# Graph attention on one core: Q rows fetched from DRAM by group, a one-hot made by a matmul of distance features, a ring of 16 gathered groups, and edge features loaded two groups at a time

## The chip, the cores and the metric

The kernel runs on one core of one Trainium2 chip. The metric is the time of one execution on the device, in microseconds (us). The kernel before takes 2109.49 us, the median of three runs (2108.01 to 2111.33). A core has five engines with instruction streams of their own: TensorE (PE; PEld is its weight load), VectorE (DVE), ScalarE (ACT), GpSimd (POOL) and SyncE (SP), which here only issues transfers. They wait for each other through semaphores.

## The reference

One graph attention layer with edge features, a residual and a layer norm. There are 6250 nodes with 128 features, 8 heads of 16, and 206250 edges sorted by their destination `dst` (33 per node on average).

```python
Q, K, V = x @ WQ, x @ WK, x @ WV            # 6250 x 128
E = edge_attr @ WE                          # 206250 x 128
score = exp(clip(sum_d(K[src] * Q[dst] * E) / 4, -5, 5))   # per edge and head
wV = segment_sum(V[src] * score, dst);  Z = segment_sum(score, dst)
out = layernorm(x + wV / (Z + 1e-6))
```

## The kernel before, in words

**Tiling.** Edges are taken in groups of 512 (4 tiles of 128), 403 groups (`G`). Nodes are cut into 49 windows of 128 (`WIN`). As the edges are sorted, a group's destinations lie close together, and the kernel finds a place for each group from its first edge: a window that starts at a multiple of 64 nodes.

**Prologue.** Twelve chunks of four windows and one of a single window. Per chunk SP loads x (`load_x`), TensorE transposes it and forms K and V (`kv_products`, L507), VectorE copies them out (`copy_kv`, L816), SP stores them to `kv_table` in DRAM (L321, L324). SP's order is: four x chunks, `dst`, two index loads (L274), four edge loads (L284), then per chunk the next x and the store. Between the copies VectorE works on `dst` (`place_first_edges`, L848; `place_groups`). TensorE turns the local destinations (`turn_local`), then forms Q chunk by chunk (`q_products`); ScalarE and VectorE split each Q chunk into three bf16 parts (L693, L832, L699, L836) kept in SBUF as `Qp`, and SP moves halves of it so that `Qp` has windows at multiples of 64 (`move_q`).

**GpSimd.** After the stores of `kv_table` it does nothing but gathers: per group four indirect transfers of 128 rows of K and V, 1 KB each (`gather`, L444), into `kv[:, g % 8]`. The ring has 8 slots (`RINGS`), and the gather of group g waits for the messages of group g - 8 (`msg_ok`).

**The main loop**, each engine in a fixed order written out in `step`:

- SP: edge features of a group, 256 KB (`load_attr`, L284; four buffers), once in eight groups the indices, once in eight groups the store of a finished window.
- TensorE, step g: turn the edge features of g+2 (`turn_attr`, L545), turn the one-hot of g+2 (`turn_hot`, L564), E of g+1 (`edge_products`, L554), Q of g+1 by the turned one-hot times three parts of `Qp` (`select_q`, L577: 12 matmuls), sums of g-1 (`sum_messages`, L588).
- ScalarE, step g: copy the turned features (L734) and the turned one-hot (L741) of g+2, the exponentials of g (L748), the one-hot of g+3 as `relu(1 - |place - node| * 2)` (`mark`, L721 four times and L726).
- VectorE, step g: K times E (L916, which waits for the gather), the sums of g-2 added to `acc` (L955 twice), times Q (L921), the messages of g-1 (L938, which reads `kv` and `msg`), the reduction to scores (L926), the clipping (L932), and in between single stages of a finished window (`finish`).

**Tail.** The last four windows are finished and stored. If a group reached beyond its place, a redo part with loops follows, which is skipped with this graph.

Of the kernel before, what the change touches and what calls it, by code (L numbers as in the profile page):

```python
# [15 lines left out]
RINGS = 8  # L16
HOTS = 5
MSGS = 2
XBUFS = 4
ATTRS = 4  # L20
LAG = 5
BIG = 1.0e6
HALF_WINDOW, SLOT, ODD_BIT, STRAYS, FIRST, OPEN = range(6)
COLUMN = (1, 3, 1)
NOT_AN_EDGE = 0.5
# [12 lines left out]
def graph_attention_layernorm(nc, x, src, dst, edge_attr, wq, wk, wv, we, out):  # L38
# [21 lines left out]
    ODD = WIN - 1  # L60
    SLOTS = WIN + ODD
# [8 lines left out]
    B_LAST = G // RINGS  # L70
    EARLY = B_LAST - LAG
    LATE = WIN - EARLY
    RES_WIN = -(-(WIN - 1) // RINGS)
    STAGES = 10 + 3 * NEWTON_STEPS
    assert STAGES <= 3 * RINGS and 0 < LATE <= TILES
# [3 lines left out]

    q_odd_dmas = sum((c * CW < ODD) + 1 for c in range(CH))  # L80

# [4 lines left out]
    kv_table = nc.dram_tensor("kv_table", [n_nodes, 2 * dim], F32).ap()  # L86

    with ExitStack() as ctx:
# [12 lines left out]
        table = sb("table", [1, 6, -(-(G + max(COLUMN)) // 4) * 4], I32)  # L101
        xT = sb("xT", [P, WIN * P])
        acc = sb("acc", [P, WIN, MW])
        Qp = sb("Qp", [P, SLOTS, 3, dim], BF16)
        kv = sb("kv", [P, RINGS, TILES, 2 * dim])
        src_idx = sb("src_idx", [P, 2, RINGS, TILES], U32)
# [3 lines left out]
        hotT = sb("hotT", [P, 2, GROUP], BF16)  # L110
        prod = sb("prod", [P, GROUP])
# [4 lines left out]
        home = sb("home", [P, GC * P])  # L116
        iota = sb("iota", [P, 2, P])
        ident = sb("ident", [P, P])
        w_e = sb("w_e", [P, dim])
        pair_col = sb("pair_col", [P, GC], I32)  # L120
        int_cols = sb("int_cols", [P, GC, 3], I32)
        place_cols = sb("place_cols", [P, GC, 3])
        home_col = sb("home_col", [P, GC])
        ones_col = sb("ones_col", [P, 1], BF16)
        one = sb("one", [P, 1])
        cur = sb("cur", [P, 2, TILES])
# [10 lines left out]
        w_kv = hot[:, XBUFS, 0:2, :].rearrange("p t d -> p (t d)")  # L137
        w_q = hot[:, XBUFS, 2, :]
        x_last = prod[:, 0:dim]
        q_rest = attrT[:, :, :]  # L140
        least = msg[:, 0, :, :].rearrange("p t m -> p (t m)")[:, 0:G]
        most = msg[:, 1, :, :].rearrange("p t m -> p (t m)")[:, 0:G]
        place_rows = hotT[0:3, :, :].rearrange("r s e -> r (s e)").bitcast(I32)[:, 0:G]
        stray_row = most[0:1, :]
        stray = prod[:, dim:2 * GROUP // 2].bitcast(BF16)[:, 0:G]
# [3 lines left out]
        rows = Qp[:, :, :, :].rearrange("p s t d -> p (s t d)").bitcast(F32)[:, SLOTS * 3 * dim // 2 - GC * GROUP:]  # L149
        dst_rows = rows.bitcast(I32).rearrange("p (c e) -> p c e", c=GC)  # L150
        local_rows = rows.rearrange("p (c e) -> p c e", c=GC)
        psT = pb("psT", [P, GROUP])
        psH = pb("psH", [P, GROUP])
# [3 lines left out]
        psX = [psT, psH]  # L157
        turn_bank = [psQ[:, 0, :], psQ[:, 1, :], psT[:, :], psH[:, :]]
# [4 lines left out]
        id_zero = sem("id_zero")  # L163
        const_ready = sem("const_ready")
# [4 lines left out]
        x_at = [sem(f"x_at{i}") for i in range(XBUFS)]  # L169
        prep = sem("prep")  # L170
        masked = sem("masked")
        turned = sem("turned")
# [6 lines left out]
        kv_out = sem("kv_out")  # L179
        kv_stored = [sem(f"kv_stored{i}") for i in range(RINGS)]  # L180
# [5 lines left out]
        q_odd = sem("q_odd")  # L186
        x_pad = sem("x_pad")
        x_res_in = sem("x_res_in")
        range_ok = sem("range_ok")
        stray_ok = sem("stray_ok")  # L190
        stray_mm = sem("stray_mm")
# [3 lines left out]
        idx_in = [sem(f"idx_in{i}") for i in range(2)]  # L195
        idx_end = sem("idx_end")
        attr_in = [sem(f"attr_in{i}") for i in range(ATTRS)]
# [7 lines left out]
        hot_tr = sem("hot_tr")  # L205
# [18 lines left out]
        s_ke = sem("s_ke")  # L224
        s_cur = sem("s_cur")
        s_hot = sem("s_hot")
        s_hot_tr = sem("s_hot_tr")
        s_hotT = sem("s_hotT")
        s_q = sem("s_q")
        s_keq = sem("s_keq")  # L230
        s_dot = sem("s_dot")
        s_clip = sem("s_clip")
        s_exp = sem("s_exp")
        s_msg = sem("s_msg")
        s_sums = sem("s_sums")
# [21 lines left out]
        def _(sp):  # L257
# [11 lines left out]
            def load_indices(b):  # L269
                if b >= 2:  # L270
                    for u in range(RINGS):
                        sp.wait_ge(kv_in[u], (b - 1) * TILES * 16)
                first, n = b * RINGS, min(RINGS, G - 1 - b * RINGS)
                sp.dma_start(src_idx[:, b % 2, 0:n, :], src[first * GROUP:(first + n) * GROUP]  # L274
                             .rearrange("(u p t) -> p u t", u=n, p=P).bitcast(U32)).then_inc(idx_in[b % 2], 16)
                if n < RINGS:
                    sp.dma_start(src_idx[:, b % 2, n, :], src[n_edges - GROUP:n_edges]
                                 .rearrange("(p t) -> p t", p=P).bitcast(U32)).then_inc(idx_end, 16)

            def load_attr(b, u):  # L280
                g = b * RINGS + u
                if past(g, ATTRS):
                    sp.wait_ge(attr_tr, g - ATTRS + 1)
                sp.dma_start(attr[:, u % ATTRS, :, :], edge_attr[bass.ds(edge0(g), GROUP), :]  # L284
                             .rearrange("(p t) d -> p t d", p=P)).then_inc(attr_in[u % ATTRS], 16)

# [11 lines left out]
            load_indices(0)  # L298
            load_indices(1)
            for u in range(ATTRS):  # L300
                load_attr(0, u)

            def move_q(c):

                w0, n = c * CW, chunk_windows(c)
                sp.wait_ge(q_lo, c + 1)
                up = min(w0 + n, ODD)
                if up > w0:
                    sp.dma_start(Qp[HALF:P, WIN + w0:WIN + up, :, :], Qp[HALF:P, w0:up, :, :]).then_inc(q_odd, 16)
# [818 lines left out]
```

## Time and profile before

| | |
|---|---|
| median of three runs | 2109.49 us (2108.01 to 2111.33) |
| the profiled execution's own time | 2111.6 us |
| its span, first to last instruction | 2109.8 us |
| mean granted TensorE clock | 0.981 of full |
| first gather starts, last starts | 47.3 us, 2086.7 us |
| bytes moved | 342.89 MB, 163 GB/s on average |
| queue of the gathers, queue of SP | 34.8% and 21.6% of 16 DMA engines |

The page gives the busy time of each engine and its share of the span, then the chain that ended last: the work followed back from the last instruction, at each step to what released it. In groups of instructions the columns are: line, engine, operation, written tile and read tiles, count, busy time and mean ns of one, then the idle time of the engine just before them and what ended most of it. "issue" is time in which an engine waited for nothing that the profile shows.

### The profile page before, as it was taken

The page shows a single profiled execution, that of the slowest core. Times are in us where ns is not written, and L with a number is a line of the kernel's source. Part 1 is how long each engine was busy: PE and PEld are TensorE (multiplying, and loading weights), DVE is VectorE, ACT ScalarE, POOL GpSimd, SP SyncE. Part 2 cuts the span into 40 slices and gives each one's busy share as a digit, 9 for nine tenths or more (in the row PEclk, how much of TensorE's full clock was granted, in tenths as well). Part 3 has the DMA queues.
Part 4 walks back from the last instruction along what each step waited for, and adds up shares of the span by engine and source line. Part 5 has one row for each costly group of instructions (what it writes and reads, how often), then busy time and mean ns, then how long its engine had stood idle before and what let it go on. Part 6 is the DMA issues. An engine that isn't in the chain of part 4 may idle for free.

```text
span 2109.8 us, 49493 instructions
## 1 busy us (share of the span) xinstructions
PE 1560.1 (74%) x14786; PEld 1436.8 (68%) x14787; DVE 1487.4 (70%) x3785; ACT 1317.4 (62%) x3270; POOL 1558.1 (74%) x1628
## 2 busy tenths in 40 slices
PE   8678777777777777777776777777777777777775
PEld 6577777677667666767666766666666667676674
DVE  4777677667767767767776776776777777677666
ACT  2667666666656666666666666666666666666663
POOL 2777777777777777777777777777777777777774
PEclk9899999989999999999999999999999999999998
DMA  7965555555555555555555555555555555555552
GB/s 236 272 176 165 161 162 161 156 158 160 154 164 157 159 162 156 161 159 158 162 159 159 157 159 160 160 161 160 157 163 158 158 162 152 162 161 159 160 156 82
DMA packets 217419, 342.89 MB, mean 163 GB/s; under 512 B 86480, under 2 KB 112056, under 8 KB 217163
## 3 DMA queue, kind: packets, MB, share of 16 engines
q0 software_dynamic: 77376, 211.39, 34.8%
q1 hardware_dynamic: 139211, 128.05, 21.6%
q8 instruction: 132, 2.16, 0.4%
q14 instruction: 124, 1.02, 0.2%
q10 hardware_dynamic: 576, 0.26, 0.0%
HBM read 325.24 MB, written 9.60 MB: 159 GB/s over the span
## 4 chain that ended last, share of the span: by engine, by line
POOL 40%; issue 20%; DVE 11%; PE 11%; DMA 8%; ACT 5%; DVEq 4%; SPq 1%; POOLq 0%
POOL kv L444 40%; DMA kv<-kv_table,src_idx 7%; PE psW L588 4%; DVE msg L938 3%; ACT hot L721 3%; DVEq L247 3%; DVE acc L955 3%; PE psE L554 2%; PE psQ L577 2%; DVE prod L921 2%; ACT hot L726 2%; PE psH L564 2%; DVE score L926 1%; DVEq L955 1%; PE psE L507 1%
## 5 line engine op out<-in xcount | busy, mean ns | idle before, releaser
L444 POOL DMA_INDIRECT kv<-kv_table,src_idx x1612 | 1549.6, 961 | 513.3 <-issue 495.7
L916 DVE TENSOR_TENSOR prod<-kv,psE 128x512 f32<-128x512 f32 x403 | 276.5, 686 | 472.9 <-DMA kv<-kv_table,src_idx 284.5
L588 PE MATMUL psW<-msg,hot 128*128 128x136 f32 x3224 | 473.6, 290 | 111.3 <-DVE msg L938 111.1
L564 PE MATMUL psH<-ident,hot 128*128 128x128 f32 x1612 | 264.8, 288 | 332.3 <-ACT hot L726 327.2
L721 ACT ACTIVATE hot<-iota,local 128x128 f32 x1612 | 508.8, 386 | 2.0 <-issue 1.5
L588 PEld LDWEIGHTS psW<-msg,hot 128*128 128x128 f32 x3224 | 406.5, 192 | 132.2 <-DVE msg L938 130.9
L564 PEld LDWEIGHTS psH<-ident,hot 128*128 128x128 f32 x1612 | 175.0, 142 | 411.3 <-ACT hot L726 410.6
L554 PE MATMUL psE<-w_e,attrT 128*128 128x128 f32 x3224 | 432.1, 278 | 0.0
L748 ACT ACTIVATE msg<-clipped 128x32 f32<-128x32 f32 x403 | 92.3, 229 | 522.4 <-DVE clipped L932 515.1
L554 PEld LDWEIGHTS psE<-w_e,attrT 128*128 128x128 f32 x3224 | 398.1, 194 | 0.0
L577 PE MATMUL psQ<-Qp,hotT 128*128 x4836 | 340.1, 221 | 8.9 <-DMA Qp<-Qp 8.9
L577 PEld LDWEIGHTS psQ<-Qp,hotT 128*128 128x128 bf16 x4836 | 308.6, 99 | 14.2 <-issue 9.2
L734 ACT ACTIVATE attrT<-psT 128x512 f32<-128x512 f32 x403 | 235.6, 585 | 114.9 <-PE psT L545 98.1
L545 PE MATMUL psT<-ident,attr 128*128 128x128 f32 x1612 | 247.3, 277 | 71.7 <-issue 71.7
L726 ACT ACTIVATE hot<-hot,one 128x512 f32<-128x512 f32 x403 | 290.8, 722 | 13.1
L955 DVE TENSOR_TENSOR acc<-psW,acc 64x136 f32 x806 | 237.7, 295 | 79.0 <-PE psW L588 68.3
L741 ACT ACTIVATE hotT<-psH 128x512 bf16<-128x512 f32 x403 | 240.2, 596 | 83.5 <-PE psH L564 81.9
L921 DVE TENSOR_TENSOR prod<-prod,psQ 128x512 f32<-128x512 f32 x403 | 277.4, 688 | 17.1 <-PE psQ L577 4.5
L938 DVE TENSOR_TENSOR msg<-kv,msg 128x512 f32<-128x512 f32 x403 | 276.9, 687 | 0.3 <-ACT msg L748 0.3
L926 DVE TENSOR_REDUCE score<-prod 128x32 f32<-128x512 f32 x403 | 271.2, 673 | 0.0
L545 PEld LDWEIGHTS psT<-ident,attr 128*128 128x128 f32 x1612 | 192.0, 143 | 80.2 <-issue 80.2
L932 DVE TENSOR_SCALAR clipped<-score 128x32 f32<-128x32 f32 x403 | 89.0, 221 | 4.6
(94 smaller groups left out, 352.7 us busy)
## 6 DMA issues: line engine op xcount, KB each, us to landing
attr<-in_edge_attr_dram SPq DMA_DIRECT2D x403, 256.0 KB
kv<-kv_table,src_idx POOLq DMA_INDIRECT x1612
kv_table<-kv SPq DMA_DIRECT2D x12, 512.0 KB, 4.0
Qp<-Qp SPq DMA_DIRECT2D x23, 192.0 KB
hot<-in_x_dram SPq DMA_DIRECT2D x12, 256.0 KB, 4.7
xT<-in_x_dram SPq DMA_DIRECT2D x8, 384.0 KB
out_dram<-xT SPq DMA_DIRECT2D x45, 64.0 KB
src_idx<-in_src_dram SPq DMA_DIRECT2D x50, 16.0 KB
```

The costliest lines, as they stand in the source:

```text
L444: nc.gpsimd.indirect_dma_start(out=kv[:, u, t, :], out_offset=None, in_=kv_table, in_offset=bass.IndirectOffsetOnAxis(ap=src_idx[:, b % 2, ...
L545: last = nc.tensor.transpose(psT[:, t * P:(t + 1) * P], attr[:, u % ATTRS, t, :], ident[:, :])
L554: last = nc.tensor.matmul(psE[:, u % 2, t * P:(t + 1) * P], attrT[:, u % 2, t * P:(t + 1) * P], w_e[:, :], start=True, stop=True)
L564: last = nc.tensor.transpose(psH[:, t * P:(t + 1) * P], hot[:, g % HOTS, t, :], ident[:, :])
L577: last = nc.tensor.matmul(psQ[:, u % 2, t * P:(t + 1) * P], hotT[:, u % 2, t * P:(t + 1) * P], Qp[:, bass.ds(slot, 1), part, :].rearrange( ...
L588: last = nc.tensor.matmul(psW[:, u % 2, 0:MW], hot[:, g % HOTS, t, :], msg[:, g % MSGS, t, :], start=(t == 0), stop=(t == TILES - 1))
L721: last = nc.scalar.activation(hot[:, g % HOTS, t, :], nodes, ACT.Abs, scale=-1.0, bias=local[:, t, bass.ds(g, 1)])
L726: nc.scalar.activation(slot, slot, ACT.Relu, scale=-1.0 / NOT_AN_EDGE, bias=one[:, 0:1])\
L921: nc.vector.tensor_tensor(prod[:, :], prod[:, :], psQ[:, u % 2, :], ALU.mult).then_inc(keq, 1)
L926: nc.vector.tensor_reduce(score[:, :], prod[:, :].rearrange("p (a d) -> p a d", d=DH), AX.X, ALU.add)\
L938: nc.vector.tensor_tensor(per_head(msg[:, g % MSGS, :, 0:dim]), per_head(kv[:, u, :, dim:2 * dim]), msg[:, g % MSGS, :, dim:MW].unsqueeze( ...
L955: last = nc.vector.tensor_tensor(where, psW[half, u % 2, 0:MW], where, ALU.add)
```

## The change

It is one change with these parts:

- `Qp` in SBUF goes. Q's three bf16 parts of a chunk are made in `q_stage` (3 buffers) and stored to `q_table` in DRAM, where the part k of node n is row 3n + k. SP loads for each group the 128 rows from its base node on (`load_near_q`, 32 KB, a ring of 4 with the address from a register): 42 nodes by 3 parts.
- The turned one-hot for Q is no longer turned from `hot`. For each edge a row of three features is stored in DRAM: n = dst - base, and n squared in two bf16 parts. One bf16 matmul with constant coefficients gives 2jn - n^2 in partition 3j + k, and ScalarE makes it a one-hot: `relu(that + 1 - j^2)`. `select_q` needs 4 matmuls, as the sum over the parts is inside the matmul. `turn_hot` goes, the one-hot for the sums is marked for g+2 (4 buffers), and edges outside of the 42 nodes are marked as strays when the features are made.
- The ring of gathered groups has 16 slots, and `src_idx` holds the indices of all groups.
- K and V are staged in `kv_stage` (4 buffers); ScalarE copies every second pair of windows.
- In SP's order, index loads and edge loads stand after the stores of chunks 9 and 10 of K and V. `acc` is zeroed by VectorE after the Q stage, not by GpSimd at the start.
- The edge features of two groups are one transfer of 512 KB into two of six buffers.

```diff
-RINGS = 8
-HOTS = 5
-ATTRS = 4
+TURN = 8
+RINGS = 16
+NEAR = 42
+QROWS = 4
+FEATS = 4
+HOTS = 4
+ATTRS = 6
@@ sync
+            def load_attr_pair(g):
+                n = min(2, G - g)
+                if g >= ATTRS:
+                    sp.wait_ge(attr_tr, g - ATTRS + 2)
+                sp.dma_start(attr[:, g % ATTRS:g % ATTRS + n, :, :], edge_attr[edge0(g):edge0(g) + n * GROUP, :]
+                             .rearrange("(u p t) d -> p u t d", u=n, p=P)).then_inc(attr_in[g // 2 % (ATTRS // 2)], 16)
+            def load_near_q(g, base):
+                if g >= QROWS:
+                    sp.wait_ge(q_sel, g - QROWS + 1)
+                sp.dma_start(q_near[:, g % QROWS, :], q_rows[bass.ds(base, P), :]).then_inc(q_in[g % QROWS], 16)
+            def load_feats(k):
+                if k >= 2:
+                    sp.wait_ge(feat_mm, (k - 1) * FEATS)
+                sp.dma_start(feats[:, k % 2, :, :], near_table[k * FEATS:(k + 1) * FEATS, :, :]
+                             .rearrange("g f e -> f g e")).then_inc(feats_in[k % 2], 16)
...
+                if c == CH - 4:
+                    for b in range(3):
+                        load_indices(b)
+                elif c == CH - 3:
+                    for g in range(0, ATTRS, 2):
+                        load_attr_pair(g)
...
+            def load_group(g):
+                nonlocal bases
+                if g >= ATTRS and g % 2 == 0:
+                    load_attr_pair(g)
+                if g % FEATS == FEATS - 1 and 2 <= (g + 1) // FEATS <= (G - 1) // FEATS:
+                    load_feats((g + 1) // FEATS)
+                if g % TURN == 0 and g // TURN + 2 <= B_LAST:
+                    load_indices(g // TURN + 2)
+                if g > QROWS:
+                    if (g - 1) % TURN == 0:
+                        bases = load_bases(g - 1, min(TURN, G - g + 1))
+                    load_near_q(g - 1, bases[(g - 1) % TURN])
@@ tensor
-                for t in range(TILES):
-                    last = nc.tensor.transpose(psH[:, t * P:(t + 1) * P], hot[:, g % HOTS, t, :], ident[:, :])
+                nc.tensor.matmul(psF[:, :], coef[:, :], feats[:, g // FEATS % 2, g % FEATS, :], start=True, stop=True)\
+                    .then_inc(feat_mm, 1)
...
-                    for part in range(3):
-                        last = nc.tensor.matmul(psQ[:, u % 2, t * P:(t + 1) * P], hotT[:, u % 2, t * P:(t + 1) * P],
-                                                Qp[:, bass.ds(slot, 1), part, :].rearrange("p a d -> p (a d)"),
-                                                start=(part == 0), stop=(part == 2))
+                    last = nc.tensor.matmul(psQ[:, g % 2, t * P:(t + 1) * P], hotT[:, g % 2, t * P:(t + 1) * P],
+                                            q_near[:, g % QROWS, :], start=True, stop=True)
@@ scalar
-                nc.scalar.activation(hotT[:, u % 2, :], psH[:, :], ACT.Copy).then_inc(hotT_ok, 1)
+                nc.scalar.activation(hotT[:, g % 2, :], psF[:, :], ACT.Relu, bias=near_bias[:, 0:1]).then_inc(hotT_ok, 1)
...
+                if CH - 8 <= c < CH - 4:
+                    near_features(c - (CH - 8))
+                elif c >= CH - 4:
+                    square_high(c - (CH - 4))
@@ vector
+            for c in range(CH):
+                copy_kv(c)
+                if c == 1:
+                    find_bases()
+                elif c == 2:
+                    find_main(0)
+                elif c == 3:
+                    find_main(1)
+                elif c == 4:
+                    keep_main()
+                elif c == 5:
+                    find_places(0)
+                elif c == 6:
+                    find_places(1)
+                elif c == 7:
+                    keep_places()
+                elif c == 8:
+                    place_groups()
```

`find_main` to `keep_places` are single operations over 128 x 2048 elements, `find_bases` four over 128 x 512 and some small ones, `place_groups` a reduction over 128 x 2048 and small ones. `near_features` is two ScalarE operations over 128 x 512, `square_high` one.

## Rows read from the trace of the kernel before

**Rows 1.** The page: engines' busy time; then the chain's shares by engine.
```profile
PE 1560.1 (74%) x14786; PEld 1436.8 (68%) x14787; DVE 1487.4 (70%) x3785; ACT 1317.4 (62%) x3270; POOL 1558.1 (74%) x1628
...
POOL 40%; issue 20%; DVE 11%; PE 11%; DMA 8%; ACT 5%; DVEq 4%; SPq 1%; POOLq 0%
POOL kv L444 40%; DMA kv<-kv_table,src_idx 7%; PE psW L588 4%; DVE msg L938 3%; ACT hot L721 3%; DVEq L247 3%; DVE acc L955 3%; PE psE L554 2%; PE psQ L577 2%; DVE prod L921 2%; ACT hot L726 2%; PE psH L564 2%; DVE score L926 1%; DVEq L955 1%; PE psE L507 1%
```

**Rows 2.** The group of L444 on the page; its durations (ns min/median/max) from its line.
```profile
L444 POOL DMA_INDIRECT kv<-kv_table,src_idx x1612 | 1549.6, 961 | 513.3 <-issue 495.7
...
L444 POOL DMA_INDIRECT kv<-kv_table,src_idx x1612: 942/946/1462, 47.3 to 2086.7; - x180
```

**Rows 3.** Timeline, last two gathers: start us, us, what, [idle before <-releaser].
```profile
2085.41 0.94 POOL L444 DMA_INDIRECT kv<-kv_table,src_idx  x1 [0.30 <-issue]
...
2086.66 1.13 POOL L444 DMA_INDIRECT kv<-kv_table,src_idx  x1 [0.30 <-issue]
```

**Rows 4.** Windows: stretch and length, PE, PEld, DVE, ACT, POOL, PEclk, DMA share, GB/s.
```profile
90.00:100.00 10.00, 8.65 (x91) 8.30 (x89) 7.09 (x15) 7.91 (x21) 7.57 (x9) 1.00 1.07 313
400.00:800.00 400.00, 299.25 (x2838) 276.13 (x2837) 283.05 (x739) 253.57 (x632) 303.69 (x317) 0.97 0.55 158
```

**Rows 5.** Waits, whole span: who waited for whom, us in total, times, longest.
```profile
DVE prod L916 <- DMA kv<-kv_table,src_idx: 284.5, 203, 4.0
...
DVE acc L955 <- PE psW L588: 68.3, 77, 2.2
...
POOL kv L444 <- DVE msg L938: 17.7, 58, 0.3
```

**Rows 6.** Timeline of the prologue.
```profile
6.43 4.95 SPq L284 DMA_DIRECT2D attr<-in_edge_attr_dram  x4
...
17.13 0.82 PE L527 MATMUL psT<-ident,hot 128*128 128x128 f32 x4 [2.07 <-DMA hot<-in_x_dram]
...
17.74 3.46 PE L507 MATMUL psE<-hot,xT 128*128 128x256 f32 x8
...
22.45 1.67 DVE L848 TENSOR_SCALAR Qp<-Qp,home_col 128x512 f32<-128x512 int32 x4
...
24.87 1.97 PE L507 MATMUL psE<-hot,xT 128*128 128x256 f32 x8 [1.07 <-DVE kv L816]
...
29.28 1.89 PE L507 MATMUL psE<-hot,xT 128*128 128x256 f32 x8
...
31.44 1.89 PE L507 MATMUL psE<-hot,xT 128*128 128x256 f32 x8
...
47.30 1.11 POOL L444 DMA_INDIRECT kv<-kv_table,src_idx  x1 [22.41 <-issue]
```

**Rows 7.** The page's groups of the turned one-hot and the Q products.
```profile
L564 PE MATMUL psH<-ident,hot 128*128 128x128 f32 x1612 | 264.8, 288 | 332.3 <-ACT hot L726 327.2
...
L577 PE MATMUL psQ<-Qp,hotT 128*128 x4836 | 340.1, 221 | 8.9 <-DMA Qp<-Qp 8.9
```

**Rows 8.** The stores of kv_table (tile kv_table): from issue to landing.
```profile
DMA to landing us min/median/max: 2.9/4.0/6.8
```

**Rows 9.** Timeline: L938, and the gather that starts while it runs.
```profile
489.69 0.68 DVE L938 TENSOR_TENSOR msg<-kv,msg 128x512 f32<-128x512 f32 x1
...
489.76 1.44 POOL L444 DMA_INDIRECT kv<-kv_table,src_idx  x1 [0.30 <-issue]
...
1005.51 0.69 DVE L938 TENSOR_TENSOR msg<-kv,msg 128x512 f32<-128x512 f32 x1
...
1006.04 0.98 POOL L444 DMA_INDIRECT kv<-kv_table,src_idx  x1 [0.30 <-issue]
```

**Rows 10.** Timeline: durations on VectorE, for the prices.
```profile
30.34 0.69 DVE L816 COPY kv<-psE 128x512 f32<-128x512 f32 x1 [0.61 <-PE psE L507]
...
71.76 0.58 DVE L885 SCALAR_TENSOR_TENSOR prod<-msg 128x403 bf16<-128x403 f32 x1
```

**Rows 11.** Windows, columns as in rows 4: a sparse stretch.
```profile
425.00:430.00 5.00, 2.88 (x16) 2.48 (x17) 4.92 (x14) 2.60 (x7) 3.78 (x5) 0.71 0.48 132
```

More of the change, by code:

```diff
@@ L358, in _ @@
                     .then_inc(x_res_in, 16)
-            for b in range(2, LAG + 2):
+            for b in range(3, LAG + 2):
                 load_turn(b)
@@ L450, in _ @@
-            for u in range(RINGS):
-                gather(0, u)
-            for b in range(1, B_LAST):
-                for u in range(RINGS):
-                    gather(b, u)
-            for g in range(B_LAST * RINGS, G):
-                gather(g // RINGS, g % RINGS)
+                        out=kv[:, g % RINGS, t, :], out_offset=None, in_=kv_table,
+                        in_offset=bass.IndirectOffsetOnAxis(ap=src_idx[:, g, t:t + 1], axis=0))\
+                        .then_inc(kv_in[g % RINGS], 16)
@@ L459, in _ @@
+            for i in range(KV_STAGES):
+                pool.wait_ge(kv_stored[i], 16 * len(range(i, CH, KV_STAGES)))
+            for g in range(G):
+                gather(g)
             pool.wait_ge(table_ok, 1)
@@ L632, in _ @@
+            select_q(0)
+            for g in range(G):
+                step(g)
+            sum_messages(G - 1)
             pe.wait_ge(table_ok, 1)
@@ L862, in _, with find_main @@
-            for pair in range(-(-WIN // 2)):
-                copy_kv(pair)
-                if pair == 7:
-                    place_first_edges()
-                elif pair == 11:
+            def find_main(half):
+                dve.wait_ge(prep, 3 + half)
+                if half == 0:
+                    nc.vector.tensor_scalar(main, near, 0.0, None, ALU.is_ge).then_inc(prep, 1)
+                else:
+                    nc.vector.scalar_tensor_tensor(main, near, float(NEAR - 1), main, ALU.is_le, ALU.mult)\
+                        .then_inc(prep, 1)
@@ L867, in _ @@
                     place_groups()
+            for c in range(GC):
+                square_low(c)
             dve.wait_ge(turned, 2)
@@ L954, in add_sums @@
                     where = acc[half, bass.ds(w, 1), :].rearrange("p a m -> p (a m)")
-                    last = nc.vector.tensor_tensor(where, psW[half, u % 2, 0:MW], where, ALU.add)
+                    last = nc.vector.tensor_tensor(where, psW[half, g % 2, 0:MW], where, ALU.add)
                 last.then_inc(added, 1)
@@ L1033, in _ @@
[L1033 to L1038 removed]
+                windows = load_windows(b * TURN - 2, TURN)
+                for u in range(TURN):
+                    step(b * TURN + u, windows[u], b - LAG)
@@ L1039, in _ @@
+            windows = load_windows(B_LAST * TURN - 2, G - B_LAST * TURN + 2)
+            for g in range(B_LAST * TURN, G):
+                step(g, windows[g - B_LAST * TURN])
+            messages(G - 1)
+            add_sums(G - 2, windows[-2])
+            add_sums(G - 1, windows[-1])
             dve.wait_ge(added, G)
```

689 lines of the change are left out of this document (332 added, 357 removed).

## The prediction

> **What bounds the kernel now.** I read the engines' shares first, then the chain that ended last, then the gathers' own group. The shares settle nothing: TensorE 74%, GpSimd 74%, VectorE 70% [rows 1]. The chain does: 40% of it is one GpSimd line, L444, the indirect gathers of K and V rows, and 20% is "issue", time in which an engine waited for nothing [rows 1]. The group of L444 says whose issue time that is: 1612 gathers of 961 ns, and before them 513.3 us of idle time, of which 495.7 us are issue [rows 2]. In the order of time the gathers start every 1.25 us: 0.94 or 0.95 us of work and 0.30 us until the next [rows 3]. Four gathers make one group of 512 edges, so GpSimd needs 5.01 us a group, 403 times. A stretch of 400 us holds 317 of them, 1.262 us apiece [rows 4]: no pause is left in it. Line L444 waited for VectorE's messages 58 times, but never over 0.3 us, which is the pause it has anyway [rows 5]. So the ring of 8 slots is never full at GpSimd's cost, from the first gather at 47.30 [rows 6] to the last at 2086.66 [rows 3]. VectorE waits for landings (284.5 us) inside a cadence that GpSimd sets [rows 5].
>
> The span is therefore three terms: 47.3 us until the first gather, 2040.5 us of gathers (2086.66 + 1.13 - 47.30), and 22.0 us of tail. The profiled execution's own time is 2111.6 for a span of 2109.8; the median of the three timed runs is 2109.49, that is 2.1 below it. I work on the span and subtract 0.3.
>
> **TensorE's and ScalarE's edits: nothing.** Per group the four turns of the one-hot (L564, 264.8 us in all) go, and the twelve Q matmuls of L577 (340.1 us in all, 0.84 us a group) become four, about 0.28 us [rows 7]. What comes is one bf16 matmul of 512 columns on 3 rows: no row has this shape; four L577 matmuls cover 512 columns in 0.28 us, and twice that is the bound for the lower clock. TensorE goes from 1560.1/403 = 3.87 us a group to 3.87 - 0.66 - 0.56 + 0.28 = about 2.9. ScalarE keeps its count: the copy of L741 becomes a Relu of the same size. None of it lies on the cadence, so its worth is 0. If the cover went it would still only help. The register loads that these two lose go to SP, once in eight groups, where 40 us stand against them.
>
> **Ring of 16, index array for all groups: nothing.** They remove a wait that costs 0 now. They do cover more: 16 groups are 80 us instead of 40.
>
> **Q rows and features from DRAM.** SP issues per group one Q load (128 rows of 256 B) and half an edge transfer, per four groups a feature load. SP's wait for a Q slot is for the Q selection four groups back, and behind it in SP's order stand edge features, indices and stores. Loads have some three groups, 15 us, to land; kv stores land in 4.0 us by the median, 6.8 at most [rows 8]. Price 0, and 0 to 1 us a group if they came late, of which VectorE's slack takes 0.9. The DMA share is 0.55 in the steady stretch and was 1.07 at 90 to 100 us, where GpSimd was busy 7.57 us in 10, as elsewhere (303.69 in 400) [rows 4]: the issue of a gather does not suffer from a full DMA system. Its landing may, by some tenths of a us, and that leads to the next term.
>
> **The stretch of the gathers: +8 us.** The gathers' median is 946 ns, their mean 961, their maximum 1462 [rows 2]. The difference is 24 us over 1612, and it has one look: a gather that starts while VectorE runs L938 (both inputs in SBUF) is stretched. Started 0.07 us after L938 it took 1.44 us; 0.53 us after, 0.98 [rows 9]. The gather seems to be held until about 0.56 us after L938 began: 0.49 us are added at 0.07, 0.03 at 0.53.
>
> The Trainium skill ("GPSIMD Engine Reference", Key points) says that GpSimd shares its SBUF interfaces with VectorE, and that instructions with two SBUF inputs contend. The trace agrees with 0.2 to 0.5 us for a hit. By the rule alone the change is neutral, since L938 is not edited; what the sum takes is from the rows.
>
> What changes is where in the 1.25 us cadence L938 falls. It starts about 2 us after L916, and L916 starts when the group's last gather has landed. Evenly spread, 0.56/1.25 = 45% of groups would be hit for 0.28 us on average: 403 x 0.126 = 51 us. Now it is 24, so the present phase is a favourable one. Extra DMA traffic shifts landings later by a little and spreads them, and VectorE loses waits of L955 for TensorE (68.3 us in 77 [rows 5]), which moves L938 earlier by 0.9 us in a fifth of the groups. Both push towards the even spread, and a lower TensorE clock (below) would too. The ends are 0 (no hit) and 113 us (all groups, 0.28 each). I take 32, a third of the way from the present value to the even spread, as it is nearest to the only measured one: +8 us.
>
> **The time to the first gather: +2.4 us.** Gathers wait for all kv_table stores. The PE pace is 2.17 us a chunk (31.44 less 29.28, rounded up) [rows 6]. Before, 4.7 us were lost to it: 2.1 of waiting for x at 17.13, 1.6 as the next products ran 3.46 us instead of 1.89, 1.1 behind VectorE's 1.67 us block at 22.45. That x load stood in SP's queue behind four edge loads that kept SP for 4.95 us from 6.43 on [rows 6]. The change moves indices and edge loads behind chunks 9 and 10, so x arrives in time, and ScalarE takes half of the copies: -4.7.
>
> Added on VectorE between the copies of chunks 1 to 8: the bases and differences 2.2 us; seven operations over 128x2048. Of these the one-input ones cost 1.2 us (0.42 per 512 columns by L848 [rows 6], 0.16 of it fixed), the others 2.3 (L885: 0.58 for 403 columns; L816: 0.69 for 512, which is also the copies' price) [rows 10]. Sum 2.2 + 3 x 1.2 + 3 x 2.3 + 3.1 for the reduction with its small ones = 15.8, with eight copies of 0.69 21.3 us against 8 x 2.17 = 17.4: +3.9. ScalarE then has two more of 0.72 (L726 is such a one) in chunks 5 to 8 and cannot begin before VectorE's fifth block ends: +1.7. So the last copy comes 0.9 us later. SP issues three index loads and three edge pairs ahead of the last two stores: 1.24 us each while the queues are full (4.95/4) [rows 6], at least some 0.4 otherwise; I take 0.8 each, 4.8 in all, of which 3.3 pass while SP would wait for the copies: +1.5. Sum -4.7 + 3.9 + 1.7 + 1.5 = +2.4. Ends: -4 (VectorE's work hidden) to +7 (the stores also queue behind 1.5 MB of edges; at the 313 GB/s of [rows 4] that is 4.8 us).
>
> **Past the first gather.** Q stage, Q stores, zeroing of acc on VectorE and the first step may end anywhere up to 80 us after the first gather. Before, all that fitted into the 40 us that a ring of 8 covers, since GpSimd never paused; the Q stores, the near loads and the features may add 5 to 10 us, and 40 more are there. Price 0.
>
> **Tail: 0.** Landing, the last two groups' sums and the late windows' stages are the same instructions; +-1 as TensorE's clock may differ.
>
> Sum: 2109.8 + 2.4 + 8 = 2120.2; less 0.3: **2120**.
>
> **Rivals.**
> Cancelling (chance 0.26): GpSimd bounds as said, but the phase stays as favourable, or the prologue gains what the stretch loses: 2105 to 2114, about 2110. For it: L938 and the gathers are untouched.
> The other side (0.22): the phase of L938 falls into the free 0.69 us of the cadence. The landing of a group decides: about 0.3 us earlier or 1 us later than now and the hits almost vanish. 24 falls to some 10 us, and the prologue gives 2: 2109.5 - 14 - 2, about 2094. For it: VectorE will be bound by landings alone, so phases may lock. Against it: the landing waits range up to 4.0 us [rows 5], too wide to lock.
> TensorE's clock (0.04): in the trace the granted clock fell to its lower level (1.2 of 2.4 GHz, shown as 0.5) in sparse stretches: 2.88 us busy in 5 and a mean of 0.71 [rows 11]. TensorE will be busy 2.9 in 5, so this comes more often. At the lower level a group needs about 6 us of TensorE, over 5.01: if it stayed there 10% of the time, 40 groups x 1 us, but the ring of 16 hides it; lasting, it would be 403 x 6 = 2418. [...]
> The Trainium skill ("TensorE: Matmul & The Clock Gate", Part 1) says that the clock follows recent activity; here that speaks against removing TensorE work, and the rows at 425 us agree.
> Q rows late (0.04): the in-order SP queue delays Q loads. From a delay of 15 us on VectorE waits; each us above its slack of 0.9 costs 403 us, so even 0.1 us above it 40: 2160.
> Not doing what it says (0.01): a group with nodes beyond 42 would go to the redo loop. A group spans 512/33 = 16 nodes, so none should.
> My forecast, stretch and prologue both a little worse, has 0.43: 2114 to 2135.
>
> **Numbers.** A change within 0.2% (2105.3 to 2113.7) is none that can be told. Faster: 0.22 and a bit of the cancelling case, 0.23; same 0.25; slower 0.43 + 0.04 + 0.04 + 0.01 = 0.52. The range leaves out the clock and Q cases above and the far part of the phase case below: 2096 to 2138.
>
> **What would show it.** The first gather at 47 to 54 us; gathers 1.25 us apart with 0.30 between; no pause of L444 anywhere; their mean at 960 to 975 ns with the median still 946; the ring wait on messages gone; TensorE at 55 to 60%. If the first gather comes before 45, the prologue step is wrong; if the mean is below 955, the phase step; if the median or the 0.30 changes, the whole argument is.

## The result, and the profile after

The changed kernel takes 2137.3 us (median of four runs, 2133.2 to 2138.8) against 2110.4 us before: a ratio of 1.012, 95% interval 1.0093 to 1.0147. It is slower, as forecast, but by more: the forecast was 2120, 17 us less, and the result lies 0.7 us inside the upper end of the range of 2096 to 2138. The profiled execution has a span of 2131.4 us (its own time is 2133.2, the lowest of the four), 21.6 us over the span before. The kernel before ran 34 times more beside the experiments; over all 38 runs its median is 2114.8 us (2106.8 to 2120.8), so the kernels are nearer 22 us apart than 27.

The page of the kernel after: engines' busy time, then the chain by engine.
```profile
PE 1589.9 (75%) x10344; PEld 1326.7 (62%) x10345; DVE 1483.1 (70%) x3784; ACT 1336.4 (63%) x3293; POOL 1569.8 (74%) x1628
...
PE 67%; issue 23%; POOL 5%; DVE 2%; DMA 2%; ACT 1%; DVEq 0%; ACTq 0%; SPq 0%; POOLq 0%
```
The group of the gathers on the page, and its durations (min/median/max) from the line.
```profile
L494 POOL DMA_INDIRECT kv<-kv_table,src_idx x1612 | 1566.1, 972 | 510.0 <-issue 482.0
...
L494 POOL DMA_INDIRECT kv<-kv_table,src_idx x1612: 942/946/1465, 52.4 to 2108.1; - x180
```
The timeline: the first gather, a gather that starts just after the messages L989 began, and the last.
```profile
52.42 1.11 POOL L494 DMA_INDIRECT kv<-kv_table,src_idx  x1 [19.25 <-DMA kv_table<-kv_stage]
...
604.55 0.68 DVE L989 TENSOR_TENSOR msg<-kv,msg 128x512 f32<-128x512 f32 x1
...
604.79 1.27 POOL L494 DMA_INDIRECT kv<-kv_table,src_idx  x1 [0.30 <-issue]
...
2108.14 1.17 POOL L494 DMA_INDIRECT kv<-kv_table,src_idx  x1 [0.30 <-issue]
```
Against [rows 2, 3, 6]: the first gather starts at 52.4 and not at 47.3 (+5.1 us), the part from the start of the first gather to the end of the last is 2056.9 and not 2040.5 us (+16.4), the tail 22.1 and not 22.0. These are the 21.6 us. The median gather is still 946 ns and the pause behind each 0.30; no pause in the whole trace is longer. Only the mean moved, 961 to 972 ns: 138 gathers take 1.01 us or more in place of 97.

Waits and a steady stretch of the kernel after (columns as in rows 5 and 4).
```profile
DVE acc L1005 <- PE psW L629: 102.8, 126, 1.8
...
POOL kv L494 <- DVE msg L989: 8.8, 29, 0.3
```
```profile
400.00:800.00 400.00, 301.91 (x1964) 252.27 (x1963) 278.94 (x734) 250.80 (x625) 304.96 (x313) 0.84 0.56 164
```
Against [rows 4]: 313 gathers in 400 us, not 317. TensorE has 1964 matmuls in place of 2838 and is busy as long, at a granted clock of 0.84 and not 0.97; over the whole kernel one matmul of L609 takes 311 ns on average where the same product, L554, took 278. The page's chain now runs through TensorE with 67%. Read alone it would say that TensorE took over as the bound. The experiments decide that.

### The profile page after: what moved, and what is told of

It reads as the page before. It is cut to its first block, busy times and chain, and to the rows that moved or that the text cites. A ratio compares the mean times of both kernels' runs of the same rounds, so it can differ in the third digit from the quotient of the medians.

```text
span 2131.4 us, 38595 instructions
## 1 busy us (share of the span) xinstructions
PE 1589.9 (75%) x10344; PEld 1326.7 (62%) x10345; DVE 1483.1 (70%) x3784; ACT 1336.4 (63%) x3293; POOL 1569.8 (74%) x1628
## 4 chain that ended last, share of the span: by engine, by line
PE 67%; issue 23%; POOL 5%; DVE 2%; DMA 2%; ACT 1%; DVEq 0%; ACTq 0%; SPq 0%; POOLq 0%
PE psW L629 24%; PE psE L609 21%; PE psT L593 10%; PE psF L601 6%; POOL kv L494 5%; PE psQ L619 4%; DMA q_table<-q_stage 1%; PE psE L555 1%; DMA near_table<-kv 1%; DVE acc L938 0%; DVEq L262 0%; DMA w_e<-in_L_gnn_WE_dram 0%; ACT kv L712 0%; DVE q_stage L852 0%; DVE attrT L848 0%
## 5 line engine op out<-in xcount | busy, mean ns | idle before, releaser
L494 POOL DMA_INDIRECT kv<-kv_table,src_idx x1612 | 1566.1, 972 | 510.0 <-issue 482.0
L629 PE MATMUL psW<-msg,hot 128*128 128x136 f32 x3224 | 580.3, 334 | 489.6 <-issue 483.1
L629 PEld LDWEIGHTS psW<-msg,hot 128*128 128x128 f32 x3224 | 499.4, 229 | 533.5 <-issue 518.3
L968 DVE TENSOR_TENSOR prod<-kv,psE 128x512 f32<-128x512 f32 x403 | 276.0, 685 | 455.2 <-DMA kv<-kv_table,src_idx 265.3
L609 PE MATMUL psE<-w_e,attrT 128*128 128x128 f32 x3224 | 523.8, 311 | 0.0
L609 PEld LDWEIGHTS psE<-w_e,attrT 128*128 128x128 f32 x3224 | 443.7, 213 | 114.3 <-issue 114.3
L755 ACT ACTIVATE hot<-iota,local 128x128 f32<-128x128 f32 x1612 | 508.7, 386 | 0.0
L1005 DVE TENSOR_TENSOR acc<-psW,acc 64x136 f32 x806 | 237.3, 294 | 112.4 <-PE psW L629 102.8
L593 PE MATMUL psT<-ident,attr 128*128 128x128 f32 x1612 | 301.7, 320 | 4.3 <-ACT attrT L766 4.3
L989 DVE TENSOR_TENSOR msg<-kv,msg 128x512 f32<-128x512 f32 x403 | 276.7, 687 | 0.3 <-ACT msg L778 0.3
L772 ACT ACTIVATE hotT<-psF,near_bias 128x512 bf16<-128x512 f32 x403 | 273.9, 680 | 0.5 <-PE psF L601 0.5
L593 PEld LDWEIGHTS psT<-ident,attr 128*128 128x128 f32 x1612 | 243.8, 169 | 4.8 <-ACT attrT L766 4.8
L601 PE MATMUL psF<-feats,coef 3*128 3x512 bf16 x403 | 179.8, 446 | 0.0
L619 PE MATMUL psQ<-q_near,hotT 128*128 128x128 bf16 x1612 | 162.6, 226 | 6.6 <-DMA q_near<-q_table 6.6
L619 PEld LDWEIGHTS psQ<-q_near,hotT 128*128 128x128 bf16 x1612 | 131.4, 103 | 13.6 <-DMA q_near<-q_table 7.1
L601 PEld LDWEIGHTS psF<-feats,coef 3*128 3x128 bf16 x403 | 37.5, 93 | 88.6 <-issue 88.6
```

Of the source, the lines that this page charges most:

```text
L494: nc.gpsimd.indirect_dma_start(out=kv[:, g % RINGS, t, :], out_offset=None, in_=kv_table, in_offset=bass.IndirectOffsetOnAxis(ap=src_idx[: ...
L593: last = nc.tensor.transpose(psT[:, t * P:(t + 1) * P], attr[:, g % ATTRS, t, :], ident[:, :])
L601: nc.tensor.matmul(psF[:, :], coef[:, :], feats[:, g // FEATS % 2, g % FEATS, :], start=True, stop=True)\
L609: last = nc.tensor.matmul(psE[:, g % 2, t * P:(t + 1) * P], attrT[:, g % 2, t * P:(t + 1) * P], w_e[:, :], start=True, stop=True)
L619: last = nc.tensor.matmul(psQ[:, g % 2, t * P:(t + 1) * P], hotT[:, g % 2, t * P:(t + 1) * P], q_near[:, g % QROWS, :], start=True, stop=True)
L629: last = nc.tensor.matmul(psW[:, g % 2, 0:MW], hot[:, g % HOTS, t, :], msg[:, g % MSGS, t, :], start=(t == 0), stop=(t == TILES - 1))
```

## The experiments

The kernel before ran beside each of them; its medians there were 2117.6 us (1 to 4), 2113.6 (5 to 8) and 2115.7 (9 to 11). Ratios are to these.

**1. Messages with one SBUF input (kernel after).** The exponentials are also written to PSUM, and the messages read them there.
```diff
+        def spread(g):
+            return psW[:, g % 2, GROUP // 2:GROUP // 2 + TILES * HEADS].rearrange("p (t h) -> p t h", h=HEADS)
...
+                nc.scalar.activation(msg[:, g % MSGS, :, dim:MW], by_head, ACT.Exp, scale=SCALE)
+                nc.scalar.activation(spread(g), by_head, ACT.Exp, scale=SCALE).then_inc(exp_ok, 1)
...
-                                        msg[:, g % MSGS, :, dim:MW].unsqueeze(3).to_broadcast([P, TILES, HEADS, DH]),
+                                        spread(g).unsqueeze(3).to_broadcast([P, TILES, HEADS, DH]),
```


> The kernel after, but ScalarE writes the exponentials a second time into PSUM, and VectorE's messages (L989) read them there, so that this operation has one input in SBUF and not two; ScalarE has one more operation of 0.23 us a group. Theory (gathers are held while the messages read two SBUF inputs): the gathers' mean falls from 972 to 947 ns, the part from first to last gather from 2057 to 2013 us, the span from 2131 to about 2088. Rival (TensorE bounds the kernel after, as its chain of waits says with 67% and a granted clock of 0.84): span 2131, gathers only later released. Rival (more DMA traffic slows gathers): mean stays at 972, span 2131.

Measured: 2095.2 us, ratio to before 0.990 (0.988 to 0.992); span 2094.3. The gathers' group, and a gather that starts 0.05 us after the messages:
```profile
L497 POOL DMA_INDIRECT kv<-kv_table,src_idx x1612 | 1528.0, 948 | 510.5 <-issue 483.4
```
```profile
136.53 0.68 DVE L993 TENSOR_TENSOR msg<-kv,psW 128x512 f32<-128x512 f32 x1
...
136.58 0.95 POOL L497 DMA_INDIRECT kv<-kv_table,src_idx  x1 [0.30 <-issue]
```
The reader is to see the same meeting of the two as above, with 0.95 us and not 1.27. The messages meet the gathers nearly as often as before, 150 in the tenths from 0.1 to 0.5 us behind L993 against 159 in the kernel after, so the phase did not move out of the way; it is the meeting that costs nothing now. The gathers take 1528.0 and not 1566.1 us in all, and the gather part falls from 2056.9 to 2019.0 us (53.5 to 2072.4). TensorE was not relieved (1567.5 us busy, clock 0.857), so it did not bound, and the DMA traffic is the same. The span is 6 us over my number: the first gather came 1.1 us later, and 1612 times 1.252 is 2019, not 2013.

**2. The same edit in the kernel before.**

> The kernel before with the same edit. Theory: mean of the gathers from 961 to 947 ns, span from 2110 to about 2084; the difference between the two kernels shrinks to that of the prologue, about 5 us. Rivals: 2110, as nothing of the DMA traffic or of TensorE is changed.

Measured: 2086.9 us, ratio 0.9865 (0.985 to 0.988); span 2083.6.
```profile
L447 POOL DMA_INDIRECT kv<-kv_table,src_idx x1612 | 1526.2, 947 | 513.2 <-issue 504.6
```
So the stretch was there before the change, and with it gone in both kernels 8.3 us are left between them (2095.2 less 2086.9; I had about 5). The gather parts are then alike (2017.0 and 2019.0 us); the rest is the first gather. Last store and first gather here, then in experiment 1:
```profile
38.31 0.35 SPq L327 DMA_DIRECT2D kv_table<-kv  x1
...
44.79 1.11 POOL L447 DMA_INDIRECT kv<-kv_table,src_idx  x1 [22.40 <-issue]
```
```profile
44.27 0.47 SPq L337 DMA_DIRECT2D kv_table<-kv_stage  x1
...
53.47 1.11 POOL L497 DMA_INDIRECT kv<-kv_table,src_idx  x1 [19.55 <-DMA kv_table<-kv_stage]
```
The runs of this kernel lie within 2.7 us of each other (2085.4 to 2088.0), those of the kernel before within 14 us (2106.8 to 2120.8). So most of what the kernel before varies by from run to run seems to be the stretch itself, and one profile of it is one sample.

**3. Messages one slot later in VectorE's order (kernel before).**
```diff
-                    if i == 1 and g >= 1:
+                    if i == 2 and g >= 1:
                         messages((g - 1) // RINGS, (g - 1) % RINGS)
```


> The kernel before with VectorE's messages issued after the reduction (L926) and not before it, in the same step. Nothing is added or taken away; L938 starts some 0.6 us later against the gathers. Theory (the phase of the messages in the gathers' cadence decides): shifting the recorded starts by 0.5 to 0.7 us puts the stretch at 50 to 68 us in place of 27, so the span grows from 2110 to 2133 to 2150, and the mean of the gathers to 975 to 987 ns. Rival (DMA traffic or TensorE): no change, 2110.

Measured: 2135.9 us, ratio 1.0093 (1.0075 to 1.0111), with the same instructions in another order.
```profile
L444 POOL DMA_INDIRECT kv<-kv_table,src_idx x1612 | 1582.7, 982 | 516.1 <-issue 503.1
```
The mean is 982 ns, 167 gathers take 1.01 us or more. The profile is of the slowest of the five runs (2146.0 us). One of GpSimd's pauses is longer here, by 2.7 us, from 86.9 us on: a wait for the first messages, as the ring is full. The medians are 18.3 us apart, far more than this pause. So the phase by itself costs: the kernel before has a favourable one.

**4. Single edge transfers (kernel after).**
```diff
-                if g >= ATTRS and g % 2 == 0:
-                    load_attr_pair(g)
+                if g >= ATTRS:
+                    load_attr(g)
```
`load_attr` moves 256 KB, with a semaphore of its own for each of six buffers.

> The kernel after with the edge features of each group as a transfer of their own (256 KB, six buffers), the rest of the change kept. Theory: bursts are shorter, but the phases are spread by all of the new traffic; the prologue issues six transfers ahead of the last stores and not three: first gather 0 to 2 us later, gathers' mean 965 to 975, span 2122 to 2136. Rival (the paired transfer makes the landings late): landings of the gathers become those of before, span 2115.

Measured: 2133.3 us, ratio 1.0083 (1.0063 to 1.0104), span 2132.4; first gather at 55.5.
```profile
L497 POOL DMA_INDIRECT kv<-kv_table,src_idx x1612 | 1563.9, 970 | 511.0 <-issue 473.7
```
Pairing the transfers is not what costs: without it the mean is 970 against 972. The first gather is 3.1 us later than in the kernel after, where I had 0 to 2; the last copy alone ended 2.2 us later.

**5. More work for TensorE (kernel after, messages from PSUM).** L601 is done four times.
```diff
-                nc.tensor.matmul(psF[:, :], coef[:, :], feats[:, g // FEATS % 2, g % FEATS, :], start=True, stop=True)\
+                for _ in range(4):
+                    last = nc.tensor.matmul(psF[:, :], coef[:, :], feats[:, g // FEATS % 2, g % FEATS, :], start=True,
+                                            stop=True)
...
```


> The kernel after with the messages read from PSUM (as in e1), and the bf16 product of coefficients and features (L601) done four times into the same bank, which is 0.65 us a group more for TensorE at 2.4 GHz and 1.3 us at 1.2 GHz. It is to keep the granted clock up and loads the engine at the same time. Theory (GpSimd's issue of gathers bounds, TensorE does not): granted clock above the 0.86 of e1 or TensorE busier, and the span as e1's, 2094, within 3 us; mean of the gathers 949 ns. Rival (TensorE bounds the kernel, chain 67%): with the lower clock kept, each group is 1.3 us longer, some 200 us in all if half of the groups are at the lower clock; with the clock back up, up to 20 us shorter than e1.

Measured: 2095.9 us (2093.5 to 2097.2) against 2095.2 in experiment 1.
```profile
L605 PE MATMUL psF<-feats,coef 3*128 3x512 bf16 x1612 | 461.4, 409 | 0.0
```
```profile
PE 1793.6 (86%) x11553; PEld 1365.8 (65%) x11554; DVE 1483.4 (71%) x3784; ACT 1385.7 (66%) x3696; POOL 1531.0 (73%) x1628
```
TensorE is busy for 226 us more than in experiment 1 and the time is the same. The clock did not come back (0.867 against 0.857). TensorE has that much room, at the clock it has, and the chain of waits, which gives it 84% here, was no sign of a bound.

**6. The prologue's order (kernel after, messages from PSUM).** The first edge pairs behind the last store, the distance features behind the last copy.
```diff
-                elif c == CH - 3:
-                    for g in range(0, ATTRS, 2):
-                        load_attr_pair(g)
+            for g in range(0, ATTRS, 2):
+                load_attr_pair(g)
...
-                if CH - 8 <= c < CH - 4:
-                    near_features(c - (CH - 8))
-                elif c >= CH - 4:
-                    square_high(c - (CH - 4))
             copy_turned()
+            for c in range(GC):
+                near_features(c)
```
(`square_high` follows `near_features` in the same way, and on VectorE `square_low` now stands behind the copy of the places.)

> The kernel after with the messages read from PSUM, and two moves in the prologue: SP issues the first edge pairs behind the last store of kv_table, and ScalarE makes the distance features after the last copy and not between the copies of chunks 5 to 12. Theory (ScalarE's features, 1.13 and 1.25 us each and not 0.72, held TensorE and the copies, and the edge pairs delayed the last store): the last copy at 37 to 39 in place of 41.5 us, the first gather at 44 to 48 in place of 52 to 53, the span shorter by just that, about 2087 against 2094. Rival (other work sets the first gather): no change. The Q stage starts some 12 us later, which costs nothing with 16 slots.

Measured: 2086.8 us, ratio 0.9884 (0.9864 to 0.9904), 8.4 less than experiment 1. The span is 2083.6, 10.7 less.
```profile
38.49 0.42 DVE L836 COPY kv_stage<-psE 128x256 f32<-128x256 f32 x1 [0.85 <-PE psE L557]
...
38.95 0.37 SPq L337 DMA_DIRECT2D kv_table<-kv_stage  x1
...
45.16 1.11 POOL L496 DMA_INDIRECT kv<-kv_table,src_idx  x1 [14.63 <-DMA kv_table<-kv_stage]
```
The last copy is 3 us earlier than in the kernel after, the last store 4.6 us, the first gather 8.3 us earlier than in experiment 1. The span follows; 2.7 us more come from the gather part (2016.3 against 2019.0), and the tail is 0.3 longer.

**7. Ring of 8 (kernel after, messages from PSUM).**
```diff
-RINGS = 16
+RINGS = 8
```

> The kernel after with the messages read from PSUM and a ring of 8 in place of 16. In the kernel after the first messages are done at 102.9 us, 50 us after the first gather, and 8 groups of gathers last 40 us. Theory: GpSimd now waits once, about 10 us, for the first messages, and hardly again, since VectorE needs 4.1 us a group to catch up against 5.0; span 2104. Rival (the ring also matters in the steady loop): over 2115. If the ring is worth nothing: 2094.

Measured: 2103.4 us (2102.8 to 2104.2), 8.2 us over experiment 1; span 2101.9.
```profile
93.05 0.95 POOL L497 DMA_INDIRECT kv<-kv_table,src_idx  x1 [0.30 <-issue]
...
103.04 0.94 POOL L497 DMA_INDIRECT kv<-kv_table,src_idx  x1 [9.04 <-DVE msg L993]
```
One pause of 9.04 us and no other. The ring of 16 is worth 8 us in this kernel, because the main loop starts later: the first L968 is at 98.7 us in the kernel after, the first L916 was at 78.7. The kernel before had almost nothing to spare here: its first messages ended at 88.6 us, 0.8 us before the gather that needs their slot could start at 89.5.

**8. The prologue's order in the kernel before (messages from PSUM).**
```diff
-            load_indices(0)
-            load_indices(1)
-            for u in range(ATTRS):
-                load_attr(0, u)
...
+                if c == CH - 5:
+                    load_indices(0)
+                    load_indices(1)
+            for u in range(ATTRS):
+                load_attr(0, u)
```
The edit also cuts the last store of `kv_table` into 96 and 10 rows, as in experiment 9.

> The kernel before with the messages read from PSUM (e2), the index loads behind the store of chunk 8, the four edge loads behind the last store of kv_table, and the last store (106 rows) cut into 96 and 10 rows. Theory: x is not held back by edge loads, which gives 3 to 5 us, and the cut store lands in 3 to 4 us in place of 6.4, so the first gather comes at 37 to 41 in place of 45 to 47, and the span falls from 2084 (e2) to about 2077. Rival: the first gather is set by VectorE's copies, 44 us, 2083.

Measured: 2086.4 us (2083.4 to 2087.4) against 2086.9 in experiment 2, which is no difference; span 2084.4, where I had 2077. The last copy ends at 37.5 us, only 0.8 us earlier than in experiment 2, and the first gather starts at 42.4 in place of 44.8 (I had 37 to 41), 4.8 us after the last store's issue began and not 6.5. But the ring of 8 is now full before the first messages are done:
```profile
83.49 0.94 POOL L449 DMA_INDIRECT kv<-kv_table,src_idx  x1 [0.30 <-issue]
...
87.01 0.95 POOL L449 DMA_INDIRECT kv<-kv_table,src_idx  x1 [2.58 <-DVE msg L944]
```
This one pause gives back what was gained.

**9. The last store cut in two (experiment 6).** The wait for this store counts both parts.
```diff
...
+                    cut = LAST_NODES // 16 * 16
+                    for lo, hi in ((0, cut), (cut, LAST_NODES)):
+                        sp.dma_start(kv_table[(WIN - 1) * P + lo:(WIN - 1) * P + hi, :],
+                                     kv_stage[lo:hi, c % KV_STAGES, 0, :]).then_inc(kv_stored[c % KV_STAGES], 16)
```

> e6 with the last store of kv_table (106 rows) cut into one of 96 and one of 10 rows. In e6 the first gather starts 6.2 us after that store is issued (38.95 to 45.16). Theory: the first gather sets all that follows, and the cut store lands in 4 us, so first gather at 42 to 43 and a span of 2081, as e6's 2083.6 less 2 to 3. Rival (the store before it lands last): no change, 2083.6.

Measured: 2084.9 us (2084.1 to 2085.5), ratio 0.9854 (0.9835 to 0.9874), span 2082.3, first gather at 41.4. The gather came 3.7 us earlier than in experiment 6. Of these, 1.2 us are a last copy that ended earlier with the same instructions before it, and 2.5 the cut: 3.7 us from the start of the issue to the gather and not 6.2. The span fell by 1.3 us only: the gather part took 2.7 us more and the tail 0.3 less. It has the lowest median here, 1.5% under the kernel before and 2.5% under the kernel after.

**10 and 11. What moves the phase.** To the kernel before is added a load of 128 rows of 256 B a group (10); or it uses only the first part of Q, 4 matmuls in place of 12 (11).
```diff
+                sp.dma_start(extra[:, n % 3, :], x[n * 15:n * 15 + P, 0:dim // 2]).then_inc(extra_in[n % 3], 16)
```
```diff
-                    for part in range(3):
-                        last = nc.tensor.matmul(psQ[:, u % 2, t * P:(t + 1) * P], hotT[:, u % 2, t * P:(t + 1) * P],
+                    last = nc.tensor.matmul(psQ[:, u % 2, t * P:(t + 1) * P], hotT[:, u % 2, t * P:(t + 1) * P],
...
```


> The kernel before with one more load for each group in SP's order, of 128 rows of 256 B from x into a buffer that nobody reads, as the Q loads of the change are. Theory a (the DMA traffic of the Q rows moves and spreads the landings, and so the phase of the messages): the stretch of the gathers grows from 29 us towards the 44 us of the kernel after, the span to 2120 to 2128. Theory b (TensorE's lighter order of work moves it): no change against before.

> The kernel before with 4 in place of 12 Q matmuls in select_q: only the first bf16 part of Q is used, the other two parts are left out. TensorE has 0.56 us a group less, no DMA is changed. Theory b (TensorE's lighter work, with its more frequent lower clock, moves the phase): stretch towards 44 us, 2120 to 2128. Theory a (the traffic does it): as before.

Measured: 10 takes 2114.1 us, ratio 0.9987 (0.9972 to 1.0002); 11 takes 2139.2 us, ratio 1.0109 (1.009 to 1.0128). Their gathers:
```profile
L450 POOL DMA_INDIRECT kv<-kv_table,src_idx x1612 | 1554.8, 965 | 513.9 <-issue 498.3
```
```profile
L444 POOL DMA_INDIRECT kv<-kv_table,src_idx x1612 | 1579.0, 980 | 513.9 <-issue 498.2
```
The traffic of the Q loads does nothing measurable; the 965 ns against 961 are one profile each, of a kernel whose runs differ by 14 us. Taking 8 small matmuls a group from TensorE, with TensorE's busy time falling from 1560 to 1446 us, makes the kernel 1.1% slower, through the mean of its gathers. It is more than the 2120 to 2128 that I had. In both profiles GpSimd waits once for the first messages, 0.7 us longer than its usual pause. The features' loads, ScalarE's new order and its longer operation for the turned one-hot (L772, 680 ns where L741 took 596) were not tested by themselves.

## Why the prediction was right, and where its sizes were off

- **How far it was right.** The direction and the bound are shown. The size is not what I forecast: +10.5 us over 2109.5, and measured +26.9 over the median taken beside it, or some 22 over the median of all 38 runs. It lies above the 2114 to 2135 of my own case, and 0.7 us inside the whole range. That it lies inside is luck in part, since both terms of the sum were too small and one rests on a cause that the experiments do not bear out.
- **The bound.** GpSimd's gathers set the time before and after. The prediction said that the median and the 0.30 us would stay and the mean rise: 946, 0.30, and 961 to 972. Shown by experiments 1 to 3 and 5: what takes the second SBUF input away brings the gathers' 1566 and 1550 us to 1528 and 1526, moving the messages alone brings them to 1583, and more work on TensorE changes nothing.
- **Lighter TensorE and ScalarE: nothing directly.** Right, and experiment 5 shows room of 226 us and more. But indirectly it costs: experiment 11. And TensorE did not get lighter as the working has it. It was to be busy for 2.9 us a group and 55 to 60% of the time; it is busy for 301.91 us in 313 gathers, 3.86 us a group, and 75%. The lower clock is one part. Another is that busy times of single lines cannot be taken off the engine's: eight Q matmuls less a group were put at 0.56 us, and experiment 11 has 0.28 (1560 less 1446 us, over 403).
- **The stretch.** The mis-sized term: +8 predicted, +16.4 measured. I had taken a third of the way to the even spread. The trace after is at it: sorted by the time from the start of L989 to the next gather, 38 of 403 in the tenth around 0.5 us, 53 around 0.9, and no tenth from 0.1 to 1.1 us below 14. Of the messages 44% have a gather that starts within 0.55 us behind them, as in an even spread; it was 32% before. My estimate for that spread was 51 us over the median, 27 more than before; the trace has 41, since a meeting costs 0.23 us on average and not 0.28.
- **Its cause was partly wrong.** I gave more DMA traffic and fewer waits of L955 for TensorE. The traffic alone gives nothing (10). The waits did not become fewer but more, 102.8 us in 126 against 68.3 in 77 [rows 5]. Nor do they follow the clock: experiment 2 has 106.2 in 134 at 0.981, experiment 4 has 73.4 in 90 at 0.864. Lighter Q matmuls alone are enough to spoil the phase of the kernel before (11), there with fewer waits (50.1 us in 60). So TensorE's share of the work can move VectorE's phase. That this is what did it in the change, which of its steps does it, and how much of it is the clock, is not shown.
- **The time to the first gather.** +2.4 predicted, +5.1 in the profiled execution. The term was too small in every profile. In this pair the last copy ended at 41.9 and not 40.8 us, +1.1 where I had +0.9. The last store was issued 1.7 us after that, behind the edge pairs, where it was at once before: +1.6 where I had +1.5. The term that was left out of the sum and stood only in its range: the first gather started 8.9 us after that issue, and not 6.5, +2.4 (the store of the kernel before is below), as the store's data queue behind 1.5 MB of edges. But this pair flatters me. The prologue of the kernel before was profiled five times (before, 2, 3, 10, 11): last copy at 38.3 to 41.0 us, first gather at 44.8 to 47.5, 46.0 on average, and the kernel before is among the late ones. That of the kernel after was profiled four times (after, 1, 5, 7): last copy at 41.8 to 44.5, first gather at 52.4 to 55.0, 53.4 on average. So the term is +7.4 us: +3.2 for the copies, +1.6 until the last store's issue, +2.6 from there to the gather. That the copies' +0.9 fits the one pair is luck: ScalarE's features took 1.13 and 1.25 us each and not 0.72, and before its last three copies VectorE sits idle 0.9 to 1.4 us for TensorE, so its added work does not set them. Experiment 6 takes the features and the edge pairs out of the way and gains 8.3 us.

The last store of the kernel before, whose first gather starts at 47.30 [rows 6]; then the kernel after, SP's queue around the last stores.
```profile
40.82 0.35 SPq L324 DMA_DIRECT2D kv_table<-kv  x1
```
```profile
37.73 2.48 SPq L286 DMA_DIRECT2D src_idx<-in_src_dram  x3
40.32 0.53 SPq L331 DMA_DIRECT2D kv_table<-kv_stage  x1
40.89 2.12 SPq L296 DMA_DIRECT2D attr<-in_edge_attr_dram  x3
43.11 0.41 SPq L331 DMA_DIRECT2D kv_table<-kv_stage  x1
43.56 0.46 SPq L334 DMA_DIRECT2D kv_table<-kv_stage  x1
```
- **Ring, Q stage, tail.** Ring of 16 at price 0: right as a sum, since the pause it avoids (9 us in 7) comes only with the change's own, later main loop, which began 20 us later and not 5 to 10. But "40 more are there" hides how close the ring of 8 was: 0.8 us were left before, and experiments 3, 8, 10 and 11 pause there for 0.7 to 2.7 us beyond the usual. Tail: 22.1 against 22.0.
- **Rivals.** TensorE's clock fell as that rival said, from 0.981 to 0.844 on average. With the messages read from PSUM it cost nothing that can be told: the gather part is 2017.0 us at 0.981 and 2019.0 at 0.857. What it does to the phase of the messages is open. The wait for the ring, which I wanted to see gone, is still listed, 8.8 us in 29 times, but never over the usual pause of 0.3. Q rows were never late enough to stop GpSimd. The phase did not fall into the free part.

## What to carry to other kernels

When one engine issues without a pause, take its mean against its median before anything else: 15 and 26 ns on 1612 instructions are 24 and 42 us, and removing the cause shortened the gather parts of the two kernels by 23.5 and 37.9 us. Here it needed an operand in PSUM in place of SBUF, for one operation of 0.18 us a group more (L783; I had taken 0.23) on an engine with room. A chain of waits that passes through an engine with 67% is not proof of a bound: give that engine more work and look. Take a start-up time from several profiles: with the same instructions it varied here by 2.7 us. A wait of 0 in a profile can be 0.8 us from being one. And in a prologue, look at what a queue issues ahead of the last transfer that others wait for: here the edge pairs held up that store's issue by 1.6 us and its landing by some 2.6.

## What the runs showed of the hardware

- A gather that starts up to some 0.5 us after a VectorE operation with two SBUF inputs of 128x512 begins is held: 1.40 us on average at 0.1 us behind, 1.29 at 0.2, 1.19 at 0.3, 1.11 at 0.4, 0.99 at 0.5 (kernel after, 159 gathers); 0.95 at each of these with one input in PSUM (experiment 1).
- Less work on an engine that does not bound made the kernel slower by 1.1% (experiment 11), and the same instructions in another order by 0.9% (experiment 3).
- The messages' product of 128x512 takes 687 ns with both inputs in SBUF (L989) and 680 with one of them in PSUM (L993, experiment 1).
- The bf16 product with 3 rows and 512 columns takes 446 ns on average at a granted clock of 0.84; in experiment 5, four in a row, 0.29 us each of busy time (461.4/1612).
- Behind a store of 106 rows the first gather started 6.2 us after its issue (experiment 6; 6.5 in the kernel before), and 8.9 us with 1.5 MB of edge loads issued just ahead of it (kernel after). Behind 96 and 10 rows it started 3.7 us after the pair of issues began at 37.7 (experiment 9).
